# Softmax sums inverted once per head instead of once per row of a tile, times-V cut in halves, new places in the order

## What is computed

```python
xn = layernorm(x)
Q, K, V = xn@wq.T, xn@wk.T, xn@wv.T          # 16 heads of 16 columns; Q and K get rotary positions
probs = softmax(causal(Q K.T / 4))           # per batch and head, 1024 x 1024
attn = (probs V) @ wo.T
g = silu((silu(xn@wg.T) * (xn@wu.T)) @ wd.T) # hidden width 768
out = x + attn * g
```

## Time and profile before

| | us |
|---|---|
| median of 3 runs | 1300.77 |
| lowest, highest | 1300.29, 1306.6 |
| the profiled execution | 1300.14 |
| its span, first to last instruction | 1298.4 |
| busy: PE | 1142.1 (88%) |
| busy: DVE | 1065.6 (82%) |
| busy: ACT | 819.4 (63%) |
| busy: POOL | 653.0 (50%) |
| granted TensorE clock, mean | 0.979 |
| DMA, mean | 117 GB/s |

### The profile page before, as it was taken

The page is one execution under the profiler, slowest core; times in us unless marked ns, Lnnn a source line. Parts: engine busy times, 40 slices in busy tenths (PEclk is TensorE's granted clock), DMA queues, the critical chain, the costliest instruction groups (busy, mean ns, idle before and its releaser), DMA issues.

```text
span 1298.4 us, 28012 instructions
## 1 busy us (share of the span) xinstructions
PE 1142.1 (88%) x9651; PEld 494.6 (38%) x9651; DVE 1065.6 (82%) x1162; ACT 819.4 (63%) x1007; POOL 653.0 (50%) x1009
## 2 busy tenths in 40 slices
PE   5989999998998888889888888888888899888873
PEld 3555565654554232233333333333323333323321
DVE  6656666657877899899999999899989999999945
ACT  4544545544444777777777677777776767767761
POOL 5666656566553222354455445454454544545442
PEclk9999999999999899999999999999999999999997
DMA  9735545576532424333443443533434244241341
GB/s 264 200 117 162 178 139 152 162 187 152 175 113 93 96 67 115 83 91 73 125 117 75 111 110 85 129 77 98 118 89 115 61 113 127 71 124 54 90 121 41
DMA packets 174265, 151.49 MB, mean 117 GB/s; under 512 B 57664, under 2 KB 150336, under 8 KB 174144
## 3 DMA queue, kind: packets, MB, share of 16 engines
q1 hardware_dynamic: 174144, 149.89, 43.1%
HBM read 72.61 MB, written 50.33 MB: 95 GB/s over the span
## 4 chain that ended last, share of the span: by engine, by line
DVE 30%; PE 28%; SPq 4%; issue 2%; DMA 2%; ACT 1%; POOL 0%; DVEq 0%; ACTq 0%; POOLq 0%
DVE mxp L832 22%; PE ps L1367 12%; PE ps L1350 7%; DVE sc L1191 7%; PE ps L810 6%; PE ps L816 2%; DMA qs<-mp 1%; SPq L1075 1%; SPq L874 1%; SPq L1074 1%; PE ps L1375 1%; ACT pr L1283 1%; DVE mneg L853 1%; DMA sc<-ot 0%; DVE mxa L841 0%
## 5 line engine op out<-in xcount | busy, mean ns | idle before, releaser
L832 DVE TENSOR_REDUCE mxp<-ps 128x2 f32<-128x1024 f32 (+2 forms) x576 | 680.7, 1216 | 71.5 <-PE ps L810 53.9
L1283 ACT ACTIVATE pr<-ps 128x1024 f32<-128x1024 f32 x576 | 574.8, 1023 | 231.3 <-PE ps L1350 220.4
L1367 PE MATMUL ps<-pr,vt 128*32 128x512 f32 (+3 forms) x3072 | 316.8, 500 | 2.3 <-POOL pr L1123 2.3
L1350 PE MATMUL ps<-qs,ks 50*128 50x512 f16 (+3 forms) x1536 | 227.8, 331 | 79.1 <-DVE mxp L832 66.0
L1123 POOL TENSOR_SCALAR_AFFINE_SELECT pr<-pr 128x256 f32<-128x256 f32 (+1 forms) x448 | 197.2, 453 | 140.6 <-ACT pr L1283 134.0
L810 PE MATMUL ps<-ks,qs 48*128 48x512 f16 (+2 forms) x1792 | 229.5, 308 | 28.1 <-ACT pr L1283 21.0
L1350 PEld LDWEIGHTS ps<-qs,ks 50*128 50x128 f16 x1536 | 69.3, 93 | 289.8 <-issue 282.6
L689 PE MATMUL ps<-xTh,wguT 128*128 128x512 f16 x384 | 145.8, 380 | 6.5 <-DVE rot L430 4.1
L810 PEld LDWEIGHTS ps<-ks,qs 48*128 48x128 f16 x1792 | 80.7, 94 | 176.9 <-issue 161.4
L689 PE MATMUL ps<-xTl,wguT 128*128 128x512 f16 x384 | 145.5, 379 | 0.0
L1191 DVE RECIPROCAL sc<-sc 128x256 f32<-128x256 f32 x64 | 111.6, 1743 | 15.3 <-DMA sc<-ot 15.3
(11 more groups left out here) (93 smaller groups left out, 1205.2 us busy)
## 6 DMA issues: line engine op xcount, KB each, us to landing
v_d<-vs SPq DMA_DIRECT2D x16, 1024.0 KB, 5.3
vt<-v_d SPq DMA_DIRECT2D x32, 512.0 KB, 4.4
xs<-in_L_attn_x SPq DMA_DIRECT2D x16, 512.0 KB, 4.7
q_parts_d<-parts SPq DMA_DIRECT2D x16, 512.0 KB, 3.0
k_parts_d<-parts SPq DMA_DIRECT2D x16, 512.0 KB, 3.1
gate_d<-gs SPq DMA_DIRECT2D x16, 512.0 KB, 3.2
qs<-q_parts_d SPq DMA_DIRECT2D x64, 128.0 KB, 3.1
ks<-k_parts_d SPq DMA_DIRECT2D x64, 128.0 KB, 3.2
```

Of the source, the lines that this page charges most:

```text
L832: dve.tensor_reduce(dst, ps[:, slot:slot + 2, :].rearrange("p t (n s) -> p (t n) s", s=w), axis=AX.X, op=ALU.max).then_inc(keep["max_dve"] ...
L1283: act.activation(probs(step, s).rearrange("p (t j) s -> p t j s", t=2)[:, :, hs[0]:hs[-1] + 1, 0:w], ps[:, slot:slot + 2, 0:w * len(hs)].r ...
L1350: ins = pe.matmul(ps[:, slot + t, o:o + w], ks[g][r, j, kb * P:(kb + 1) * P], qs[g][r, j, lo:lo + w], start=o == 0, stop=True, skip_group_ ...
L1367: ins = pe.matmul(ps[VW * j:VW * (j + 1), O0, lo - c * CH:CH], vt[g % 2][:, kb, j, :], probs(step, s)[:, j, at:at + w], start=first, stop= ...
```

## The change

The softmax sums no longer go to `sc` by way of four 16-partition copies per half group. One DMA per half group stores the four rows of sums to DRAM (`raw_d`). When a batch's four groups are through, the 16 x 512 sums of a half are loaded as 128 x 64 (`fetch_sums`), inverted by one instruction of VectorE, stored to DRAM (`store_sums`), and in the next group loaded into `sc` by 16 DMAs, one per head, each repeating a row over 16 partitions (`load_sums`). The last group keeps the old way, with an inversion of 64 x 128 elements per tile. Nine of the ten times-V steps may be cut into two halves by columns, each at a turn of its own (`V_PARTS`). `ORDER` and most places are new numbers. The mask tables are made for partitions 0 to 63 in GpSimd's first gaps, and two DMAs copy them to partitions 64 to 127.

```diff
-                low_tokens(pool, (0, 0))
+                ch(pool.memset(pick[:, :], 0.0))
+                ch(pool.memset(future[:, :], 0.0))
+                mask_runs(RUNS[:2])
+                low_tokens(pool, (0, 0))
+                mask_runs(RUNS[2:])
+                mask_leaves(0, 1)
...
                     if is_first(step):
-                        constants()
-                    for t in range(2):
-                        if isinstance(step[0], int) and step == MASK_MADE[t]:
-                            mask_factors(t)
+                        mask_leaves(1, LEAF - 1)
+                        ch(pool.memset(exp_table[:, :], 0.0))
...
+                    if isinstance(step[0], int) and step == MASK_MADE:
+                        sp.wait_ge(s_c, MASK_STEPS)
+                        for table in (pick, future):
+                            sp.dma_start(table[TILE:P, :], table[0:TILE, :]).then_inc(keep["s_mask"], 16)
...
-        ORDER = "EMEMEMEMEMEMEMMEMEMEMEMEMEMEMEMEMEEM"
+        ORDER = "EMEEMEMEMEMEMEMEMEMEMEMEMEMEMEMEMMEM"
...
-            V_AT = (13, 16, 18, 24, 30, 33, 35, TURNS + 2, TURNS + 5, TURNS + 8)
-            late = [s for s in range(NSTEP) if V_AT[s] >= TURNS]
-            TAKE1, TAKE0, MAXT, NEG, SPLIT_AT = 5, 8, 25, 12, 11
-            INVERT, HALVE, ADD = (0, 3), (1, 6), (7, 13)
-            WO, MUL = (11, 21), (7, 10)
+            V_AT = (10, 13, 13, 20, 26, 30, 32, 35, TURNS + 2, TURNS + 4)
+            V_HALF_AT = (10, 15, 15, 23, 28, 32, 35, TURNS + 1, TURNS + 5, TURNS + 7)
+            V_PARTS = []
+            for s in range(NSTEP):
+                if V_AT[s] == V_HALF_AT[s]:
+                    V_PARTS.append((s, None, V_AT[s]))
+                else:
+                    V_PARTS += [(s, 0, V_AT[s]), (s, 1, V_HALF_AT[s])]
+            late = [(s, part) for s, part, at in V_PARTS if at >= TURNS]
+
+            def half_pieces(pieces, width, part):
+                mid, out = width // 2, []
+                for kb, lo, at, w in pieces:
+                    a, z = max(at, part * mid), min(at + w, mid + part * mid)
+                    if a < z:
+                        out.append((kb, lo + a - at, a, z - a))
+                return out
+            TAKE1, TAKE0, MAXT, NEG, SPLIT_AT = 4, 9, 26, 12, 12
+            INVERT, HALVE, ADD = 16, (0, 5), (4, 15)
+            WO, MUL = (8, 18), (5, 10)
...
-            TAKE1_LAST, TAKE0_LAST = 2, 8
+            TAKE1_LAST, TAKE0_LAST = 3, 8
...
+            def sums_of(step):
+                b, g = step
+                if g == (NG - 2 if b == B - 1 else NG - 1):
+                    return b, 0
+                return (b - 1, 1) if g == 0 and b else None
+
+            def sum_rows(b):
+                return (H - GH if b == B - 1 else H) * 8
...
                         sp.dma_start(oc[b % 2][r:r + DK, g // 2, c * CH:(c + 1) * CH], ot[o:o + DK, c]).then_inc(o_in[b % 2][c], 16)
-                        sp.dma_start(sc[b % 2][r:r + DK, g // 2, c * CH:(c + 1) * CH], ot[o + DK:o + VW, c]).then_inc(o_in[b % 2][c], 16)
+                        if step == LAST:
+                            sp.dma_start(sc[b % 2][r:r + DK, g // 2, c * CH:(c + 1) * CH], ot[o + DK:o + VW, c]).then_inc(o_in[b % 2][c], 16)
+                    if step != LAST:
+                        sp.dma_start(raw_d[b, c, g * GH:(g + 1) * GH], ot[DK:P:VW, c]).then_inc(o_in[b % 2][c], 16)
+
+                def fetch_sums(b, c):
+                    n = sum_rows(b)
+                    sp.wait_ge(*landed((b, n // 8 // GH - 1), c))
+                    sp.dma_start(sums[c][0:n, :], raw_d[b, c, 0:n // 8].rearrange("h (i e) -> (h i) e", i=8)).then_inc(o_raw[c], 16)
+
+                def store_sums(b, c):
+                    n = sum_rows(b)
+                    sp.wait_ge(o_inv[c], b + 1)
+                    sp.dma_start(sums_d[b, c, 0:n // 8].rearrange("h (i e) -> (h i) e", i=8), sums[c][0:n, :]).then_inc(o_sst[c], 16)
+
+                def load_sums(b, c):
+                    if b > 1:
+                        sp.wait_ge(t_norm.sem, t_norm.after((b - 2, (c + 1) * CT - 1)))
+                    sp.wait_ge(o_sst[c], (b + 1) * 16)
+                    for h in range(sum_rows(b) // 8):
+                        r = h * DK % P
+                        sp.dma_start(sc[b % 2][r:r + DK, h * DK // P, c * CH:(c + 1) * CH],
+                                     sums_d[b, c, h:h + 1].to_broadcast([DK, CH])).then_inc(o_sld[c], 16)
...
                             load_v(nth(step, 1))
+                        if sums_of(nth(step, -1)):
+                            load_sums(*sums_of(nth(step, -1)))
...
                     move_output(step, 0)
+                    if sums_of(step):
+                        fetch_sums(*sums_of(step))
...
                         load_max(sp, keep, nth(step, 1))
+                    if sums_of(step):
+                        store_sums(*sums_of(step))
...
                 def scale_tile(tile):
-                    pool.wait_ge(t_rec.sem, t_rec.after(tile))
+                    b, t = tile
+                    pool.wait_ge(*landed((b, NG - 1), t // CT))
+                    pool.wait_ge(o_sld[t // CT], (b * H + sum_rows(b) // 8) * 16)
...
-                        for i, tile in enumerate(output_tiles(step)):
-                            if n == INVERT[i] and tile:
-                                invert_sums(tile)
+                        if n == INVERT and sums_of(step):
+                            invert_sums(*sums_of(step))
...
-                        for s in range(NSTEP):
-                            if V_AT[s] == n:
-                                times_v(step, s)
+                        for s, part, at in V_PARTS:
+                            if at == n:
+                                times_v(step, s, part)
...
```

More of the change, by code:

```diff
@@ L906, in attention_phase @@
         sc = [sb(f"sc{i}", [P, KD, S], F32) for i in range(2)]
+        sums = [sb(f"sums{c}", [P, CH // 8], F32) for c in range(HALVES)]
+        raw_d, sums_d = (nc.dram_tensor(n, [B, HALVES, H, CH], F32).ap() for n in ("raw_d", "sums_d"))
+        o_raw = [sem(f"o_raw{c}") for c in range(HALVES)]
+        o_inv = [sem(f"o_inv{c}") for c in range(HALVES)]
+        o_sst = [sem(f"o_sst{c}") for c in range(HALVES)]
+        o_sld = [sem(f"o_sld{c}") for c in range(HALVES)]
         gt = sb("gt", [P, HALVES, CT, D], F32)
@@ L1103, in _ @@
                 load_output(B - 1, 1)
+                fetch_sums(B - 1, 1)
+                store_sums(B - 1, 1)
+                load_sums(B - 1, 1)
                 move_output(LAST, 1)
@@ L1186, in _, with invert_sums, invert_last @@
                 t_rec.start(dve)
-                def invert_sums(tile):
+                def invert_sums(b, c):
+                    n = sum_rows(b)
+                    dve.wait_ge(o_raw[c], (b + 1) * 16)
+                    dve.reciprocal(sums[c][0:n, :], sums[c][0:n, :]).then_inc(o_inv[c], 1)
+                def invert_last(tile):
                     b, t = tile
-                    dve.wait_ge(*landed((b, NG - 1), t // CT))
-                    dve.reciprocal(columns(sc, tile), columns(sc, tile)).then_inc(t_rec.sem, 1)
+                    dve.wait_ge(*landed(LAST, t // CT))
+                    part = columns(sc, tile)[P - GH * DK:P, KD - 1:KD]
+                    dve.reciprocal(part, part).then_inc(t_rec.sem, 1)
                 def group(step, prev):
@@ L1247, in last_group @@
                         result(i)
[L1248 to L1251, removed]
+                    sums(3)
+                    sums(4)
+                    result(3)
+                    sums(5)
+                    result(4)
+                    sums(6)
+                    invert_sums(B - 1, 1)
+                    result(5)
+                    result(6)
                 over_groups(group, last_group)
                 for tile in end_tiles:
-                    invert_sums(tile)
+                    invert_last(tile)
                     scale_tile(tile)
@@ L1352, in keys_by_queries, with times_v @@
                     ins.then_inc(st_pe.sem, 1)
-                def times_v(step, s):
+                def times_v(step, s, part=None):
                     b, g = step
                     c, pieces, width = STEPS[s]
+                    if part is not None:
+                        pieces = half_pieces(pieces, width, part)
                     first, last = s in (0, HALF_STEPS), s in (HALF_STEPS - 1, NSTEP - 1)
-                    if s == 0:
-                        pe.wait_ge(v_ld[g % 2], b * 32 + 16 * (g // 2) + 16)
-                    if first:
-                        pe.wait_ge(o_act.sem, o_act.after(*((step, 1) if c else (earlier(step, 1), 2))))
-                    if diagonal(s):
-                        pe.wait_ge(causal.sem, causal.after(step, sum(len(diagonal(EXPU[u][0])) for u in diag_units if EXPU[u][0] <= s)))
-                    pe.wait_ge(expo.sem, expo.after(step, last_of[s] + 1))
+                    if part != 1:
```

(20 more changed lines are left out.)

50 lines of the change are left out of this document (26 added, 24 removed).

## The result

The changed kernel takes 1350.72 us (median of four runs, 1347.56 to 1359.63) against 1300.53 for the kernel before (four runs, 1300.18 to 1306.6): a ratio of 1.0386, 95% interval 1.0327 to 1.0444. It is slower, as forecast, by 50 us where 14 were forecast, and lies 0.7 us outside the range. The profiled execution took 1347.56 us with a span of 1345.8, which is 47.4 longer than before (1300.14, span 1298.4).

A forecast was written before the change was run, and what follows sets the result against it. The prediction took VectorE to bound the attention phase, with two inversions per group on top of the maxima. Masks, ordinary groups, stall, lateness and the rest summed as 1300.14 - 8 - 65 + 73 + 13 + 1 = 1314 us, range 1268 to 1350.

The forecast's parts named there:

- the low clock behind the stall: TensorE after its wait in group (b, 0): the prediction had no term for a lower clock there.
- the lateness in (b, 2): First turn after group (b, 1) waits 1.8 us for `load_max` behind sixteen loads, seven times: +13 us.
- Masks: Projection chunks held up by mask selects, 3.3 and 4.7 us: both delays go, -8 us, bounds -9 and -4.
- The ordinary group: Attention phase: period falls from 26.72 to 24.3 us with TensorE the heavier engine, -65 us over 27 distances.
- The stall in (b, 0): TensorE waits 10.4 us at the wo product for sums from sixteen loads, in seven batches: +73 us.
- The lower bound: Smallest stall in (b, 0): copy at 6.0, issue every 0.41, landing 2.0, TensorE at 12.9 give 6.8 us (+48).
- That is in the -65: SyncE's three fewer DMAs per half take away the late `load_max` behind (b, 3), counted within the ordinary groups' -65 us.
- The last group: Twice 12 loads against fewer moves and smaller inversions at the end: +2 us, between -4 and +10.
- B: Rival: SyncE issues the sixteen loads faster; at 0.3 us per load the kernel takes 1285 us; chance 0.23.
- C: Rival: TensorE loses more by halves and new places, period 25.5 us, -33 in place of -65: 1342; chance 0.13.
- D: Rival: loads issue at the moves' 0.63 us, 17.5 us of waits per batch: 1351; chance 0.13.
- E: Rival: the wait in (b, 0) doesn't bite because `sc` is there in time: 1228; chance 0.07.

The follow-up runs named there:

- the filled wait: The changed kernel with 44 unused matmuls ahead of the wo product in the seven groups (b, 0): 1341.99 us, ratio 1.0273 to the kernel before.
- The last experiment: New sums and masks, two loads ahead of the moves, old ORDER, places and whole times-V steps; in (b, 3) gate and x loaded behind `load_max`: 1225.07 us, 0.9394.

## Why the prediction was wrong

The direction and the mechanism were right, the size was not: +50 in place of +14. Two steps failed: the low clock behind the stall was put at nothing (12.5 us), and the lateness in (b, 2) at 13 us in place of 29. With both, the sum of 1314 would have been 1342.

- **Masks**, -8: right. 6.6 in the trace up to the first joined maxima, 7.4 alone by the ratio.
- **The ordinary group**, 24.3 us and -65: right. Measured 24.2 and -69. The 0.7 us put on TensorE for the halves lies between the two comparisons, 23.28 against 23.10 in this trace and 23.52 against 22.43 without the halves. The Trainium skill's sixty cycles per matmul ("TensorEngine Tiling (Array Packing)", Instruction Overhead) would have been 1.8, above both.
- **The stall in (b, 0)**, 10.4 us seven times: right, 9.9, in part by luck. The order of SyncE's work and its price per move were readable ahead. Four errors of about 1 us cancelled in batch 3: a load took 0.52 instead of 0.46, but the moves began 0.8 sooner and the last load landed about 1 us faster (median 1.9 in the list of DMA issues, for the 3.2 taken), and TensorE arrived 0.8 sooner. The lower bound's own terms give 7.0, not 6.8.
- **The clock behind the stall**: no term in the sum, and the step that failed first. The sum ended a wait where the wait ends. The clock cost 1.8 us more per turn, 12.5 us, shown by the filled wait. The groups (b, 0) came to 36.9 where 34.7 was forecast.
- **Lateness in (b, 2)**, 1.8 us seven times: mis-sized, 4.2, which is 29 us in place of 13. The wait itself was 2.9. Sixteen loads at a mean of 0.53 instead of 0.46 are the 1.1 us between that and the forecast; `load_max`, at 0.60 to 0.88 for the 0.61 taken, adds some in four batches. The rest, 1.3, stands behind the wait, where the clock is lower; how much of it the clock costs wasn't tried. Two loads instead of sixteen took all of the lateness away.
- **The first turns of (b, 0)** were a further 0.3 to 1.9 us late in six batches, 7.2 in all, with the gate and x loads of (b, 3) ahead of `load_max`. "That is in the -65" was wrong for these. The last experiment shows at the old places that it is the order on SyncE; in the changed kernel itself it wasn't tried.
- **The last group**, +2: 5.7. TensorE waited 9.89 us for `aT` once, behind the twelve loads (5.46 us) and the moves queued after them, where it had waited 6.31 before. With two loads in place of the twelve, and nothing else new, it waits 5.22 and the whole stretch is 66.2 us, 0.2 over the kernel before; so this excess is SyncE's issuing too. That an inversion of 64x128 took 0.95 us, where half of 1.74 was reckoned, is 0.6 us in all. The product's row in the changed kernel, in the one with two loads and in the kernel before:

```profile
1308.37 1.44 PE L1467 MATMUL ps<-woT,aT 128*128 128x256 f16 x6 [9.89 <-POOL aT L1205]
```
```profile
1265.21 1.44 PE L1467 MATMUL ps<-woT,aT 128*128 128x256 f16 x6 [5.22 <-POOL aT L1205]
```
```profile
1263.68 1.44 PE L1375 MATMUL ps<-woT,aT 128*128 128x256 f16 x6 [6.31 <-POOL aT L1136]
```

By these terms the traces' 47 are the 14 forecast, +16 in (b, 0), +16 in (b, 2), -4 in the ordinary groups, +4 at the end and +1 for the masks. The 16 in (b, 0) are 12.5 for the clock, -3.3 for the somewhat shorter stall, and 7 left over, which is what the late first turns waited.

Of the rivals, B (fast issues) fails at once: 0.47 to 0.58 per load. C (a period of 25.5) fails by the measured 24.2. D had the time nearly right, 1351, for a wrong reason: the loads didn't take 0.63. Its time came about by a missing term of 12.5 and one that was half its size; the range, which ended at 1350, left out even D's own time. For E, the wait that doesn't bite, I forecast 1228; two loads ahead of the moves are that case, 1238. The DRAM loads at 0.46 that stand against B are of the attention phase, not of the projection phase. The Trainium skill's sentence on a small sequencer time ("DMA: Bandwidth & Descriptors", Issuing engines are not separate DMA queues) holds for one load and fails for sixteen: 8.37 us of issuing stand before 1.9 of landing.

## What to carry to other kernels

Data that goes out to DRAM and comes back is priced at the queue of its issuing engine: count every DMA between the copy and the last load, times the interval of that queue, and compare with the turn at which the consumer arrives. Ahead of that, look for the one wider DMA that replaces the row of small ones and for an earlier place, since either alone gave back only part. And a wait of 10 us on TensorE costs more than its length: add what the half clock takes behind it, here 1.8 us.

## What the runs showed of the hardware

- The granted clock stayed at half for 3.5 to 5.7 us after each of seven waits of 9.5 to 10.3 us, though TensorE was busy again. At a first turn, nine waits were between 1.7 and 4.2 us long: seven of them, from 1.82 us on, had 0.61 us E units behind them, those of 1.73 and 2.92 had none. Keeping TensorE busy with unused matmuls through the wait kept it at full clock.
- A row of sixteen 32 KB loads: 0.47 to 0.58 us of issue each and, in batch 3, 1.65 us from the last issue's end to the use. Two 256 KB ones: 0.65 each, and 5.5 us behind `vt`'s 512 KB, 4.2 us without it ahead (718.00 + 1.34 to 723.53). The bytes in all are the same, 512 KB. While GpSimd waited for the two in batch 3, the DMA share was 0.58 to 0.59; what makes the landing longer was not tried.
- Issues of the same four 4 KB transfers took 0.61 to 0.91 us each in the kernel before, and 0.60 to 0.88 behind sixteen loads and five moves in the changed one. So the sixteen loads aren't what it hangs on; why isn't settled.
